# Last step and epilogue of a windowed-attention kernel rebuilt: the last half's attention first, later layers in its gaps

## What is computed

```python
# layer 0, on windows of 8x8 pixels (16 per image, 64 tokens each, 8 heads of 16)
normed = layernorm(win, ln1_g, ln1_b)
q, k, v = split(normed @ in_w.T + in_b)
o = softmax(q @ k.T / sqrt(16)) @ v            # per window and head
y = win + (o @ out_w.T + out_b)
y = y + silu(layernorm(y) @ fc1_w.T + fc1_b) @ fc2_w.T + fc2_b     # hidden 256
# layer 1, on the 1024 pixels of an image, E = 64, no softmax
q, k, v = wq @ x + bq, wk @ x + bk, wv @ x + bv
out = wo @ ((q @ k / 1024) @ v) + bo + x
```

## Time and profile before

| what | us |
|---|---|
| median of 3 runs (lowest to highest) | 370.13 (368.29 to 372.71) |
| profiled execution, its own time | 369.95 |
| its span, first to last instruction | 368.1 |
| PE busy in the span | 345.6 (94%) |
| DVE / ACT / POOL busy | 285.2 / 246.1 / 166.7 |
| last odd step on PE | 323.2 to 343.3 |
| epilogue | 343.3 to 368.1 |

### The profile page before, as it was taken

How to read it: one execution, slowest core, us unless ns; L and a number is a source line. 1 busy time by engine, 2 the same in 40 slices (tenths; PEclk the granted TensorE clock), 3 DMA queues, 4 the chain that set the end, 5 groups by cost and what they waited for, 6 DMA issues and landing times.

```text
span 368.1 us, 9773 instructions
## 1 busy us (share of the span) xinstructions
PE 345.6 (94%) x3349; PEld 296.1 (80%) x3349; DVE 285.2 (77%) x850; ACT 246.1 (67%) x449; POOL 166.7 (45%) x177
## 2 busy tenths in 40 slices
PE   4798999999999999999999999999999999999764
PEld 3588888888888888888888888888888888879552
DVE  5666788898788878798788878898788888777552
ACT  5557677675958577675968667684968658673550
POOL 6506175545455434635446434636445533522430
PEclk9998999999999999999999999999999999999996
DMA  4224030403222131302223031312123030200101
GB/s 132 63 67 109 8 95 16 104 13 73 73 68 72 28 86 57 86 29 71 71 63 80 21 93 57 78 36 64 53 81 87 14 100 32 66 22 2 59 1 57
DMA packets 31714, 21.98 MB, mean 60 GB/s; under 512 B 22416, under 2 KB 23504, under 8 KB 31696
## 3 DMA queue, kind: packets, MB, share of 16 engines
q1 hardware_dynamic: 31696, 21.75, 21.6%
HBM read 4.95 MB, written 4.19 MB: 25 GB/s over the span
## 4 chain that ended last, share of the span: by engine, by line
PE 80%; issue 5%; DVE 5%; ACT 4%; SPq 2%; POOL 1%; DMA 1%; DVEq 0%; ACTq 0%; POOLq 0%
PE p_scoreT L685 13%; PE p_c L576 12%; PE p_score L666 10%; PE p_attn L704 9%; PE p_a L576 6%; PE p_a L648 4%; PE p_scoreT L689 4%; PE p_c L762 4%; PE p_d L576 3%; DVE xn_tok L1183 3%; PE p_a L627 3%; PE p_c L733 2%; PE p_a L617 2%; PE p_c L720 2%; PE p_c L739 2%
## 5 line engine op out<-in xcount | busy, mean ns | idle before, releaser
L495 POOL TENSOR_TENSOR hid_l<-hid,hid_h 128x512 fp32r<-128x512 f32 x30 | 40.4, 1367 | 41.0 <-ACT hid_h L1041 39.1
L666 PE MATMUL p_score<-kd_h,qd_h 128*128 128x128 f32 (+1 forms) x512 | 56.4, 253 | 1.1 <-issue 1.0
L1236 DVE TENSOR_REDUCE row_max<-p_score 128x8 f32<-128x512 f32 x64 | 44.0, 687 | 15.4 <-PE p_score L666 15.4
L666 PEld LDWEIGHTS p_score<-kd_h,qd_h 128*128 128x128 f32 (+1 forms) x512 | 50.9, 166 | 6.0 <-issue 1.3
L1007 ACT ACTIVATE probs<-p_scoreT 128x512 f32<-128x512 f32 x64 | 38.6, 603 | 23.8 <-PE p_scoreT L689 23.5
L500 POOL TENSOR_TENSOR y_l<-y,y_h 128x512 fp32r<-128x512 f32 (+1 forms) x17 | 20.7, 1217 | 68.8 <-ACT y_h L1021 68.8
L704 PEld LDWEIGHTS p_attn<-vd,probs 128*64 128x64 f32 x1024 | 36.3, 140 | 17.3 <-issue 10.3
L704 PE MATMUL p_attn<-vd,probs 128*64 128x34 f32 x1024 | 45.3, 244 | 2.4 <-ACT probs L1007 2.0
L487 POOL TENSOR_SCALAR kd_l<-k_l,head_a 128x512 fp32r<-128x512 f32 x15 | 23.6, 1572 | 38.4 <-DVE k_l L1218 24.1
L685 PE MATMUL p_scoreT<-qd_h,kd_h 128*128 128x256 f32 x128 | 39.5, 309 | 0.0
L479 POOL TENSOR_TENSOR rstd<-rstd,minus_half 128x4 f32<-128x4 f32 (+1 forms) x33 | 35.5, 1075 | 2.7
(11 more groups left out here) (195 smaller groups left out, 903.4 us busy)
## 6 DMA issues: line engine op xcount, KB each, us to landing
qd_h<-q_h SPq DMA_DIRECT2D x64, 64.0 KB, 2.0
qd_l<-q_l SPq DMA_DIRECT2D x64, 64.0 KB, 2.0
vd<-v_tok SPq DMA_DIRECT2D x64, 64.0 KB, 2.2
out<-out_sb SPq DMA_DIRECT2D x16, 256.0 KB, 2.0
x_in<-in_x SPq DMA_DIRECT2D x14, 256.0 KB, 2.7
x_first<-in_x SPq DMA_DIRECT2D x2, 256.0 KB, 2.8
fc_rows<-in_L_conv_fc_w SPq DMA_DIRECT2D x2, 128.0 KB, 2.6
in_w_rows<-in_L_conv_in_w SPq DMA_DIRECT2D x1, 192.0 KB, 2.6
```

Source lines behind the costliest of these rows:

```text
L495: pool.tensor_tensor(hid_l[:, t], hid[:, t], hid_h[:, t].bitcast(F32), ALU.subtract).then_inc(hid_low[t], 1)
L666: last = pe.matmul(p_score[0:rows, 2 * KEYS * j:2 * KEYS * (j + 1)], qd_h[:, h.par, j, 2 * KEYS * p:2 * KEYS * p + rows], kd_h[:, h.par, 2 ...
L1236: dve.tensor_reduce(row_max[:, p % 2], p_score[:].rearrange("row (h k) -> row h k", h=HEADS), AXIS_X, ALU.max).then_inc(max_ready[p], 1)
```

## The change

Only the last odd step and the epilogue are changed; `step_odd(last)` goes and each engine's epilogue holds both. On each engine the order is written out anew:

- Attention of the last half goes first. D of image 6 (`d_kvT`, `d_bT`, `d_mT`, both `d_final`) moves from within it to behind it, and so does the early part's projection. The early part's transpose moves from ahead of `b_attn(b, 2)` to ahead of `b_attn(b, 3)`.
- The late part gets banks of its own, `p_score` and `p_scoreT`, and the two parts go through C side by side, with `c_fc2` and `c_kv` of half 0 and D of image 6 between their stages. Their y2 has a buffer of its own, `y2_last`.
- D of the last image uses `p_attn` for kvT, bT and mT, in place of `p_d`.
- POOL takes the rstd of half 0 ahead of the low part of y2 of half -1, not behind it.
- ACT takes `c_o` of both parts behind the four silu instructions of half 0, `yn_h` of the late part ahead of the early part's silu, and `d_out` of image 6 between them.
- The last products: half 0 starts on m_h alone and its third pass waits for m_l; half 1 is done in two products of 256 columns into `p_a[0]` and `p_a[1]`, each read by one DVE instruction and stored by a DMA of 128 KB of its own.

The core of the diff, in the order of the file: the helpers and `images`, then SP's epilogue, PE's new `d_final_last`, the head of POOL's epilogue, and DVE's `d_out_last`.

```diff
         def c_banks(h):
-            return p_a if h.early else p_c
+            return p_a if h.early else [p_score, p_scoreT] if h.late else p_c
+        def y2_of(h):
+            return y2_last if h.early or h.late else y2
+        def d_bank(loop, c):
+            return p_attn if isinstance(loop.i, int) and loop.i + c == IMAGES - 1 else p_d
...
             step_even(last, more=False, c=True)
-            step_odd(last, more=False, d=True)
             epilogue(last)
...
             def epilogue(loop):
-                store(loop, 0)
+                store(loop, -1)
+                dst = out.rearrange("b c (h v row) win -> b h v c (row win)", h=2, v=2)[IMAGES - 1]
+                sp.wait_ge(fin_kept[0], IMAGES)
+                sp.dma_start(out.rearrange("b c (h row) win -> b h c (row win)", h=2)[IMAGES - 1, 0], out_sb[:, 0, :]
+                             ).then_inc(out_dma[0], 16)
+                sp.wait_ge(fin_first_kept, 1)
+                sp.dma_start(dst[1, 0], out_sb[:, 1, 0:HALF // 2]).then_inc(out_dma[1], 16)
+                sp.wait_ge(fin_kept[1], IMAGES)
+                sp.dma_start(dst[1, 1], out_sb[:, 1, HALF // 2:HALF]).then_inc(out_dma[1], 16)
...
+            def d_final_last(loop):
+                pe.wait_ge(m_high, IMAGES)
+                pe.wait_ge(y2_low, loop.halves(0))
+                pe.wait_ge(fin_kept[1], IMAGES - 1)
+                pe.matmul(p_d[:], m_h[:], y2_h[:, 0], start=True, stop=False)
+                pe.matmul(p_d[:], m_h[:], y2_l[:, 0], start=False, stop=False)
+                pe.wait_ge(m_low, IMAGES)
+                pe.matmul(p_d[:], m_l[:], y2_h[:, 0], start=False, stop=True).then_inc(fin_ready[0], 1)
+                pe.wait_ge(d_kept, IMAGES)
+                for v, done in ((0, fin_first_ready), (1, fin_ready[1])):
+                    part = slice(v * HALF // 2, (v + 1) * HALF // 2)
+                    three_passes(p_a[v][:, 0:HALF // 2], [(m_h[:], m_l[:])], [(y2_h[:, 1, part], y2_l[:, 1, part])]
+                                 ).then_inc(done, 1)
...
                 early, late = Part(loop, 0), Part(loop, 1)
+                rstd2_of(loop.half(0))
+                y2_low_part(loop.half(-1))
+                hidden_low(loop.half(0), 0)
+                hidden_low(loop.half(0), 1)
+                rstd2_of(early)
                 rstd2_of(late)
...
-                dve.wait_ge(fin_ready[1], loop.image(0))
                 dve.wait_ge(out_dma[1], loop.image(-1, times=16))
-                for v in range(2):
-                    last = dve.tensor_scalar(in_rows(out_sb[:, 1, :], v), in_windows(p_a[0][:], v), d_col[:, 0:1],
-                                             None, ALU.add)
-                last.then_inc(fin_kept[1], 1)
+                for v, ready, kept in ((0, fin_first_ready, fin_first_kept), (1, fin_ready[1], fin_kept[1])):
+                    dve.wait_ge(ready, IMAGES if v else 1)
+                    dve.tensor_scalar(in_rows(out_sb[:, 1, :], v), in_windows(p_a[v][:], 0), d_col[:, 0:1],
+                                      None, ALU.add).then_inc(kept, 1)
```

More of the change, by code:

```diff
@@ L89 @@
 class Half:
-    tiles, cols, early = range(4), slice(0, HALF), False
+    tiles, cols, early, late = range(4), slice(0, HALF), False, False
     def __init__(self, loop, c):
@@ L122, in __init__ @@
         super().__init__(loop, 1)
-        self.part, self.early = part, part == 0
+        self.part, self.early, self.late = part, part == 0, part == 1
         self.tiles, self.cols = range(2 * part, 2 * part + 2), slice(part * HALF // 2, (part + 1) * HALF // 2)
@@ L214, in build @@
         y2 = sb("y2", [C, HALF])
+        y2_last = sb("y2_last", [C, HALF])
         y2_h = sb("y2_h", [C, 2, HALF], F32R)
@@ L556, in step_odd @@
             def step_odd(loop, more, d):
-                step(loop, loop.half(1), more, more, True, d, not more)
+                step(loop, loop.half(1), more, more, True, d)
             def epilogue(loop):
                 early, late = Part(loop, 0), Part(loop, 1)
+                rstd2_of(loop.half(0))
[3 more added lines that the diff above has]
+                rstd2_of(early)
                 rstd2_of(late)
@@ L715, in c_transpose @@
                     pe.wait_ge(k_low, 2 * IMAGES)
-                elif h.follows(1):
+                elif h.follows(1) and not h.late:
                     pe.wait_ge(hid_high[0], h.n(1))
@@ L744, in c_fc1 @@
                 pe.wait_ge(yn_low, h.n())
-                if t == 1 and not h.early:
+                if t == 1 and not h.early and not h.late:
                     if h.follows(1):
@@ L769, in d_kvT @@
                 pe.wait_ge(kv_kept, loop.halves(c) - 1 if tiles[-1] < 7 else loop.halves(c))
-                if loop.follows(c - 1):
+                dst = d_bank(loop, c)
+                if loop.follows(c - 1) and dst is p_d:
                     pe.wait_ge(fin_kept[1], loop.image(c - 1))
@@ L1110, in step @@
                     c_silu(c, 1)
-                if not with_last:
-                    c_o(b)
-                if with_d and not with_last:
+                c_o(b)
+                if with_d:
                     d_out(loop, -1, 1)
@@ L1119, in step_odd @@
             def step_odd(loop, more, d):
-                step(loop, loop.half(1), more, more, True, d, d, not more)
+                step(loop, loop.half(1), more, more, True, d, d)
             def epilogue(loop):
                 early, late = Part(loop, 0), Part(loop, 1)
+                b, c, tail = loop.half(1), loop.half(0), loop.half(-1)
+                load_exp_table(b)
+                b_exp(b, 0)
+                b_widen(b, 2)
+                b_exp(b, 1)
+                c_y2(tail)
+                b_exp(b, 2)
+                c_yn(c)
+                b_exp(b, 3)
+                load_silu_table(b)
+                c_silu(c, 0)
+                c_silu(c, 1)
+                c_o(early)
                 c_o(late)
-                d_out(loop, -1, 1)
                 c_yn(early)
-                c_y2(loop.half(0))
+                c_y2(c)
+                d_out(loop, -1, 0)
+                c_yn(late)
                 c_silu(early, 0)
                 c_silu(early, 1)
-                c_yn(late)
                 c_silu(late, 0)
                 c_silu(late, 1)
+                d_out(loop, -1, 1)
                 c_y2(early)
```

157 lines of the change are left out of this document (98 added, 59 removed).

## The result

The changed kernel takes 367.89 us (median of 15 runs, 366.03 to 368.48), the kernel before 371.45 us in its 15 runs beside them. One of those 15 took 531.74 us and stands outside the comparison. The ratio is 0.9916, with a 95% interval of 0.9895 to 0.9937: 0.84% less. The forecast was 367.1 us, by its own sum 0.77% less, with a range of 365.4 to 369.2. It counted from a profiled execution of 369.95 us, and the median of the kernel before came out at 371.45. So the gain is larger than forecast and the time is 0.8 us above it.

What follows compares the result with a forecast made beforehand. The last odd step was taken as bound by PE (TensorE), the epilogue by a chain of short stages. 3.3 - 0.35 - 0.9 + 0.7 + 0.1 = 2.85 us off 369.95 gave 367.1 us; range 365.4 to 369.2.

Steps and rivals of the forecast that it cites:

- A: Until the end of attention: PE work taken out of the PE-bound stretch ends attention 3.3 us earlier, bounds 2.3 and 3.5.
- B: From attention's end to the hidden layer's last low part: changed queue orders cost 0.35 us, bounds 0 and 1.0.
- C: From the hidden layer's last low part to mT of the last image: 0.9 us longer, bounds 0.5 and 1.2.
- D: The last products, mT to last output: m_l off the path and a shorter last output gain 0.7 us.
- I keep half: The last products: TensorE's clock was taken as half, 0.43 us for 512 columns against 0.23 at full clock.
- first rival: The last products: the clock stays full, 1.1 us less, 366.0 us; chance 0.18.
- E: The last store: 128 KB in place of 256 gains 0.1 us, bounds 0 and 0.4.
- The three issues don't queue up: The last stores: no queueing among their three issues, since the outputs are 0.6 us apart.
- second rival: Attention: its uncovered chain costs 1 us and low parts on VectorE and POOL meet, 0.4; 368.5 us; chance 0.15.
- slower rival: Epilogue: the clock falls early in the new one, 6.7 us more, 373.8 us; chance 0.05.
- full-clock rival: Same as the first rival: full clock for the last products, 1.1 us less, 366.0 us; chance 0.18.

## Why the prediction was right

**A, forecast 3.3, measured 3.30 us.** Both halves of its reasoning stand: PE's work counts one for one there (0.92 for 0.93), and the rstd's new place keeps the next wait away (1.45 us without it). The forecast named this wait but gave it no price; it is almost half of A. That the number fits to 0.01 is luck: the pieces summed up to 3.48 were 3.24 us of busy time, and the 0.2 us taken for new waits did not come.

**B, forecast -0.35, measured -0.44.** The queue delays on ScalarE and VectorE are there: yn_h of the late part starts 9.2 us behind attention for the forecast's 9.1. But the first of them, o_h 0.3 us late (forecast 0.46), was made up for by the statistics; the loss arises at the late norm, 0.77 us (forecast 0.5). The low passes moved there cost nothing, because a path of equal length runs beside them. That mT and the output of image 6 cost the 0.44 us is argued.

**C, forecast -0.9, measured -0.88.** One line takes it back.

**D, forecast 0.7.** The split is worth 0.81 at equal clock. The profile has 1.01 (4.58 to 3.57), because the clock fell later within the last products than before. How late varies: the profile with kv first has 3.49 us, the second one of the kernel before 4.50. It is low for the whole of them in other runs: 4.06 us with the new end, 4.87 with the old. "I keep half" was right for most of the products; the first rival's full clock came only with work put into the waits.

**E, forecast 0.1, measured 0.01.** The number fits, the reasoning does not. "The three issues don't queue up" left out the transfers, which do: the last 128 KB stand behind 384 KB on busy DMA engines, where the last 256 KB of the kernel before had them to themselves. That the two come out alike is luck as far as known.

**The sum** is 3.30 - 0.44 - 0.88 + 1.01 + 0.01 = 3.00 us for 2.85. By itself the total of 367.89 us proves little, since the unchanged start alone varies by 2.6 us and the old epilogue's clock may add to the difference of the medians. The steps carry it. The second rival did not come: no wait on attention's chain, and the low part of y2 of half 0 on GpSimd ended 0.5 us ahead of the first low part on VectorE, which took 0.42 us. The slower rival had its mechanism right and its side wrong: it hits the old epilogue, and its price was smaller, 0.9 us for 3.4 us of low clock and 1.5 us for twice that. The full-clock rival's "1.1 less, 366.0 us" was mis-sized for the whole: from mT to the output 1.14 us do go (4.06 to 2.92), but 0.4 to 0.6 come back as a longer store. A term was missing from it, the DMA engines as bound of the end.

## What to carry to other kernels

Ask of each stage what ends it, and move work from the one bound by an engine into the waits of the one bound by a chain: here the products taken out gave 3.30 us, and the stage that took them in became 0.44 us longer. Look then for the wait that the moved work had hidden, and for the order of the short chain behind it; a producer of the late part should not stand behind a consumer of the early one. Compare profiles from the same instruction on when the clock at the start differs, and with the last stores check the DMA engines before buying speed for the last products.

## What the runs showed of the hardware that was not expected

Most of the spread of the runs came from TensorE's clock: 2.6 us of it arise in the first 40 us, at two waits, and ten short products in them ended it. The first wait, for the spread q, ends at 18.3 to 18.5 us in every profile, but its length varies. In the five profiles where the clock fell behind it, it was 1.75 to 2.01 us; in the changed kernel's own it was 1.28, and the clock stayed at 1.00. The second, for the fourth exponential, is 1.12 to 1.14 us wherever no product was put in, and the clock fell at it in nine of 13 profiles. At the end, the last image's stores of 512 KB keep the DMA engines busy for 1.5 us. With outputs ready within 0.5 us the last one ends 3.05 us behind its output for 2.46; another issuing queue does not help.
